# An encoder behind an expert attention on one core: the opening overlapped, the weights in five parts, and a new order of each engine's work in a slot

## What is computed

```
n = layer_norm(x0)
e = n + experts(n)            # 8 heads; a quarter of the rows each uses the first 128, 64, 32, 16 values
x = n
for i in range(4):
    q, k, v = split(layer_norm(x) @ Wi.T + bi)
    scores = q @ k.T / sqrt(8) + mask     # 16 heads, causal, with bias
    x = x + softmax(scores) @ v @ Wo.T + bo
    h = gelu(layer_norm(x) @ W1.T + b1)
    x = x + h @ W2.T + b2
return x0 + layer_norm(x) + e
```

## Time and profile before

| | us |
|---|---|
| Runs: median (lowest to highest) | 1649.23 (1647.62 to 1650.16) |
| Profiled execution: its own time | 1640.9 |
| Profiled execution: first to last instruction (span) | 1639.1 |
| PE busy / PE weight loads busy | 1421.8 / 946.2 |
| ACT busy | 1223.2 |
| DVE busy | 1131.8 |
| POOL busy | 614.3 |

### The profile page before, as it was taken

How to read it: one execution, slowest core, us unless ns; L and a number is a source line. 1 busy time by engine, 2 the same in 40 slices (tenths; PEclk the granted TensorE clock), 3 DMA queues, 4 the chain that set the end, 5 groups by cost and what they waited for, 6 DMA issues and landing times.

```text
span 1639.1 us, 38563 instructions
## 1 busy us (share of the span) xinstructions
PE 1421.8 (87%) x10720; PEld 946.2 (58%) x10720; DVE 1131.8 (69%) x2851; ACT 1223.2 (75%) x2165; POOL 614.3 (37%) x1052
## 2 busy tenths in 40 slices
PE   0677787568999999999999999999999989999995
PEld 0445554335666666666666666666666656666653
DVE  6567676347777777677677766777776767777762
ACT  3233333238999898898999888999888988888884
POOL 5232222123333343333333333334333345555443
PEclk9999888779999999999999999999999999999997
DMA  3332333045444444444444445444444444444430
GB/s 107 100 114 89 107 92 101 24 122 149 121 124 127 117 116 126 134 129 119 120 129 119 122 121 133 129 119 121 127 119 123 129 128 125 124 125 125 123 90 10
DMA packets 104789, 187.60 MB, mean 114 GB/s; under 512 B 19912, under 2 KB 70728, under 8 KB 104720
## 3 DMA queue, kind: packets, MB, share of 16 engines
q1 hardware_dynamic: 89904, 150.45, 33.3%
q0 software_dynamic: 14848, 36.72, 8.3%
HBM read 120.87 MB, written 65.01 MB: 113 GB/s over the span
## 4 chain that ended last, share of the span: by engine, by line
PE 53%; DVE 17%; issue 14%; DMA 9%; POOL 2%; DVEq 1%; ACT 1%; SPq 1%; POOLq 0%; ACTq 0%
PE pvp L979 11%; PE exp_ps L956 7%; DVE negm L698 6%; PE mxp L923 6%; PE dense L1009 6%; PE dense L1018 5%; PE dense L868 5%; DMA blocks<-split_L 4%; PE mxp L927 4%; DVE xn L666 3%; PE dense L896 2%; PE dense L997 2%; DVE ost L744 2%; PE mxp L868 2%; DMA blocks<-negt 2%
## 5 line engine op out<-in xcount | busy, mean ns | idle before, releaser
L831 ACT ACTIVATE probs<-exp_ps 128x512 f32<-128x512 f32 x896 | 525.0, 593 | 289.1 <-PE exp_ps L956 286.4
L698 DVE TENSOR_REDUCE negm<-mxp 128x2 f32<-128x512 f32 x896 | 569.2, 683 | 90.3 <-PE mxp L927 72.6
L956 PE MATMUL exp_ps<-qbd_l,kst_l 128*128 128x512 f32 x768 | 368.5, 495 | 8.3 <-issue 4.3
L923 PE MATMUL mxp<-blocks,qst 104*128 104x512 f32 x768 | 325.5, 453 | 34.5 <-DMA blocks<-split_L 19.7
L855 ACT ACTIVATE exp_ps<-masktf 128x512 f32<-128x512 f32 x513 | 308.8, 602 | 22.6 <-DVE rest L766 6.5
L927 PE MATMUL mxp<-maskb,identb 128*128 128x256 bf16 (+1 forms) x768 | 247.6, 322 | 0.0
L498 POOL TENSOR_SCALAR veps<-mv 128x2 f32<-128x2 f32 x144 | 31.7, 220 | 560.9 <-DVE mv L657 557.2
L923 PEld LDWEIGHTS mxp<-blocks,qst 104*128 104x128 f32 x768 | 149.0, 194 | 84.2 <-DVE negm L698 37.0
L979 PE MATMUL pvp<-probs,vst_l 128*32 128x256 f32 (+1 forms) x4096 | 194.5, 330 | 0.6 <-ACT probs L831 0.6
L744 DVE COPY ost<-pvp 128x512 f32<-128x512 f32 x80 | 55.3, 692 | 201.6 <-PE pvp L979 201.6
L956 PEld LDWEIGHTS exp_ps<-qbd_l,kst_l 128*128 128x128 f32 x768 | 144.4, 195 | 40.8 <-issue 31.3
(11 more groups left out here) (95 smaller groups left out, 2006.6 us busy)
## 6 DMA issues: line engine op xcount, KB each, us to landing
split_L<-hi SPq DMA_DIRECT2D x256, 128.0 KB, 2.1
qst<-split_L SPq DMA_DIRECT2D x64, 384.0 KB
kst_l<-split_L SPq DMA_DIRECT2D x64, 384.0 KB
qbd_l<-split_L SPq DMA_DIRECT2D x256, 96.0 KB
split_L<-lo POOLq DMA_DIRECT2D x128, 128.0 KB, 2.1
blocks<-split_L SPq DMA_DIRECT2D x128, 96.0 KB
blocks<-split_L POOLq DMA_DIRECT2D x128, 96.0 KB, 4.4
split_F<-hi SPq DMA_DIRECT2D x64, 128.0 KB, 2.1
```

What stands on the lines that cost most here:

```text
L698: dve.tensor_reduce(heads[:, g, first:first + count], mxp[:, (plan.max_chunks * g + ch) % 3, :].rearrange("p (h t) -> p h t", h=count), AX ...
L831: act.activation(probs[:, g[0], ch, :], exp_ps[:, (plan.exp_chunks * g[0] + ch) % 2, :], ACT.Exp, scale=plan.scale).then_inc(q.b_exp, 1)
L923: pe.matmul(mxp[:, bank, :], qst[0:BIAS_END, g[0], qt * P:(qt + 1) * P], kbd[0:BIAS_END, first:first + count, g[0], 0:keys], start=True, s ...
L956: pe.matmul(exp_ps[:, bank, :], kst[plan.name][:, s, g[0], kt * P:(kt + 1) * P], rhs, start=not on_diagonal, stop=True, skip_group_check=T ...
```

## The change

Nothing is computed otherwise, and the instructions that compute are the same in number (one memset of a single column goes). Four things change.

1. **The order in a slot.** `slot_steps` of the encoder is rewritten. Steps that several engines shared under one name are split, so that each engine's part has a place of its own: `qk+` into y (ACT), hi (DVE), lo (POOL), hi> (SP); `ln` into ln and rstd; `f1+` into two gelus; `f2` into two halves; `negt+` and `stack...` into the issuing engines' steps. The statistics and `xn` now belong to unit s+3, `v` stands at the end of the slot before, and the copy `pv+` is made one slot later. The maxima stand beside the exponentials 4 to 11, before beside 2 to 8.
2. **Banks.** Each transient result of PE has a bank of its own choice among five (`banks`), and a bank's reader is waited for by a helper (`take`).
3. **Weights in five parts**, each loaded as soon as its own last use is over; the first layer's are loaded at the start of the program. The columns of the two weight tiles are sorted to suit.
4. **The opening.** Before the last expert slots, each engine now runs the early steps of the encoder's first units (statistics of units 0 and 1, projections of unit 0). `blocks` is cleared after the last expert exponential, no longer after the last expert unit, and only some engines wait for the end of the experts.

```
         if self.causal:
             end, end2, store = (at(k, s - 2) if last_layer else [] for k in ("end", "end+", "store"))
             return (
-                exps[0:2] + at("ot", s - 1) + at("ln", s + 2) + at("ot+", s - 1) + at("v v+", s + 1) + at("xn", s + 2)
-                + at("f2 f2+", s - 2) + at("at at+", s - 1)
-                + exps[2:3] + maxes[0:2] + at("xt", s + 2)
-                + exps[3:4] + maxes[2:4] + at("xt+", s + 2) + at("op", s - 1) + at("stack+", s + 1)
-                + exps[4:5] + maxes[4:5] + at("op+", s - 1) + at("qk", s + 2)
-                + exps[5:6] + maxes[5:7] + at("qk+", s + 2)
-                + exps[6:7] + maxes[7:9] + at("xn2", s - 1) + end
-                + exps[7:8] + maxes[9:11]
-                + exps[8:9] + maxes[11:12]
-                + exps[9:10] + at("xt2 xt2+", s - 1) + values[0:2] + end2
-                + exps[10:11] + at("negt negt+", s + 1) + at("stack_max+", s + 2)
-                + exps[11:12] + at("f1 f1+", s - 1) + values[2:4] + at("pv+", s) + store)
+                at("rstd", s + 3) + part("f2", s - 2, 0) + at("ln", s + 3)
+                + part("exp", s, 0) + at("v+", s + 1) + at("w:v", s + 2)
+                + part("exp", s, 1) + at("ot pv+", s - 1) + part("f2", s - 2, 1) + at("w:w2 at+ ot+ at w=w1", s - 1)
+                + part("exp", s, 2) + at("stack>", s + 1) + at("xt", s + 2)
+                + part("exp", s, 3) + at("w=o op", s - 1) + at("hi>", s + 2) + at("row>", s + 1) + at("f2+", s - 2) + end
+                + part("exp", s, 4) + at("op+", s - 1) + part("max", s + 1, 0) + at("w=v xt+", s + 2) + part("pv", s, 0)
+                + part("max", s + 1, 1, 2) + at("w=w2", s - 1)
+                + part("exp", s, 5) + at("xn2", s - 1)
+                + part("exp", s, 6) + part("max", s + 1, 3, 4) + at("smax> qk y", s + 2) + at("w:qk", s + 3)
+                + part("exp", s, 7) + at("xt2", s - 1) + part("max", s + 1, 5) + at("xb xt2+", s - 1) + at("hi", s + 2)
+                + part("exp", s, 8) + part("max", s + 1, 6) + part("pv", s, 1) + part("max", s + 1, 7)
+                + part("exp", s, 9) + at("rstd2", s - 1) + part("max", s + 1, 8, 9) + end2 + part("max", s + 1, 10)
+                + part("exp", s, 10) + at("lo", s + 2) + part("max", s + 1, 11) + at("w=qk", s + 3)
+                + part("exp", s, 11) + part("gelu", s - 1, 0, 1) + part("f1", s - 1, 0) + at("negt negt+", s + 1)
+                + part("f1", s - 1, 1) + at("w:w1", s) + part("pv", s, 2) + at("smaxp", s + 2) + at("xn", s + 3)
+                + at("xb2", s - 1) + at("w:o", s) + part("pv", s, 3) + at("v", s + 2) + store)
...
+            if early is not None and early != (step in EARLY or step[0] == "w"):
+                continue
...
+ENCODER = Plan("L", 16, True, True, LAYERS * BATCH // 2, {
+    "xt": 1, "qk": 0, "v": 3, "at": 2, "op": 4, "xt2": 1, "negt": 2, "f2": 1, "ot": 4, "f1": (0, 1)})
+EARLY = ("ln", "rstd", "xn", "xt", "xt+", "qk", "y", "hi", "lo", "hi>", "v", "v+")
...
+WEIGHTS = {
+    "qk": ("a", A_Q, A_V), "v": ("a", A_V, A_COLS),
+    "o": ("c", C_O, C_W1), "w1": ("c", C_W1, C_W2), "w2": ("c", C_W2, C_COLS)}
...
+def wait_for_projections(eng, q):
+
+    for done in (q.a_rstd, q.a_xn, q.a_xt, q.a_mask, q.a_qk, q.a_v, q.a_hi, q.a_lo):
+        eng.wait_ge(done, EXPERT.units)
+    for s in range(2):
+        eng.wait_ge(q.parts[s], 16 * 4 * EXPERT.rounds)
+        eng.wait_ge(q.lo_parts[s], 16 * 2 * EXPERT.rounds)
+
+
+def expert_rounds(eng, experts, encoder, join):
+
+    experts(-1)
+    experts(0)
+    experts(1)
+    with eng.Fori(2, EXPERT.rounds - 1) as n:
+        experts(n)
+    experts(EXPERT.rounds - 1, slots=(0,))
+    join()
+    encoder(-2, early=True)
+    encoder(-1, slots=(0,), early=True)
+    experts(EXPERT.rounds - 1, slots=(1,))
+    experts(EXPERT.rounds)
+
+
+def encoder_opening(encoder, experts_done=None):
+
+    encoder(-2, early=False)
+    encoder(-1, slots=(0,), early=False)
+    if experts_done is not None:
+        experts_done()
+    encoder(-1, slots=(1,))
+    encoder(0)
+    encoder(1)
```

More of the change, by code:

```diff
@@ L114, in steps @@
+    def steps(self, n, last_layer=False, slots=(0, 1), early=None):
+        for step, off, *k in sum((list(self.slot_steps(s, last_layer)) for s in slots), []):
             u = 2 * n + off
+            if early is not None and early != (step in EARLY or step[0] == "w"):
+                continue
             if not isinstance(n, int) or 0 <= u < self.units:
-                yield step, u, off % 2, n + off // 2, g, off
-EXPERT = Plan("F", 8, False, False, BATCH // 2)
+                yield step, u, off % 2, n + off // 2, k[0] if k else 0, off
@@ L419, in load_c, with load_weights @@
-            def load_c(layer):
-                sp.wait_ge(q.c_done, BATCH * (layer + 1))
-                settle(sp, passed_sp)
-                sp.dma_start(wc["L"][:], wc_l[layer]).then_inc(q.wc, 16)
-                sp.wait_ge(q.wc, 16 * (layer + 1))
+            def load_weights(part, layer):
+                which, first, end = WEIGHTS[part]
+                to, source = (wa["L"], wa_l) if which == "a" else (wc["L"], wc_l)
+                sp.dma_start(to[:, first:end], source[layer][:, first:end]).then_inc(q.w[part], 16)
@@ L465, in _ @@
+            encoder_round(LAYERS - 1, 0)
+            encoder_round(LAYERS - 1, 1, last_layer=True)
+            with sp.Fori(2, per - 2) as k:
+                encoder_round(LAYERS - 1, k, last_layer=True, inner=True)
+            for k in range(per - 2, per + 1):
+                encoder_round(LAYERS - 1, k, last_layer=True)
             for s in range(2):
@@ L1023, in run @@
-            def run(plan):
-                read = [None, None]
-                def body(n):
-                    steps(plan, n, read)
-                    for k in range(2):
-                        if read[k] is not None:
-                            before, per_round, constant = read[k]
-                            read[k] = (before, per_round, constant - per_round)
-                rounds_of(pe, plan, body)
+                        o = take(at["f1"][k], q.c_gelu, NF, off, 2 * k + 2)
+                        for f in range(2 * k, 2 * k + 2):
+                            last = pe.matmul(o[:, (f % 2) * T:(f % 2 + 1) * T],
+                                             wc["L"][:, C_W1 + f * P:C_W1 + (f + 1) * P], xnt[:, 1, s, :],
+                                             start=True, stop=True)
@@ new lines, in next_round, with experts @@
+            def next_round(n):
+                for number, job in enumerate(read):
+                    if job is not None:
+                        before, per_round, constant = job
+                        loop_follows = not isinstance(n, int) or n == 1
+                        read[number] = ((before, per_round, constant - per_round) if loop_follows else
+                                        (before, 0, per_round * n + constant))
+            def experts(n, **part_of_round):
+                steps(EXPERT, n, **part_of_round)
+                next_round(n)
@@ L1036, in _, with encoder @@
+            def encoder(n, **part_of_round):
+                steps(ENCODER, n, **part_of_round)
+                next_round(n)
             pe.wait_ge(s_init, 12)
```

529 lines of the change are left out of this document (284 added, 245 removed).

## The result

| | before | after |
|---|---|---|
| Median of 4 runs each, us | 1648.4 (1644.1 to 1650.2) | 1679.7 (1672.5 to 1680.5) |
| Ratio to before, 95% interval | | 1.0181 [1.0153, 1.021] |
| Span of the profiled execution, us | 1639.1 | 1678.0 |

The kernel is 1.8% slower; the forecast was 1564.5, and the range ended at 1630. (A fourth run of the kernel before puts its median at 1648.4, for 1649.2 in the first table.) First the page of the changed kernel: its span, and the clock granted to TensorE in 40 slices, in tenths.

What follows compares the result with a forecast made beforehand. Each slot was DVE's stretch (10.37 us), then PE's queue (7.79), 18.26 with register rows; savings of 57.6 in three layers, 1.8 after unit 0, 13.7 in the last layer and 11.6 opening took 1649.2 to 1564.5; range 1525 to 1630.

Steps and rivals of the forecast that it cites:

- Each of the last 14 keeps its 0.94: 19.20 for 20.18: Last layer's 14 slots, with the final norm: each stays 0.94 us over a middle slot, together 13.7 us saved.
- The wait for the weights goes: Layer starts: weights in five parts arrive in time, leaving 3.0 of 6.6 us of other delays a layer.
- The slot: Encoder's middle slot: two stretches in turn plus 0.1 for register rows, 18.26 us, before 19.24.
- The DVE stretch: From the sum through the last maximum, DVE nearly without a break: work kept, left at 10.37 us.
- the other: From the last maximum to the next sum, set by PE's queue: 7.79 us, before 8.87.
- PE needs 17.5 and has little reserve: PE's work in a slot, priced from start to start: about 17.5 us, its busy 18.38 taken as overstated.
- Register arithmetic, 0.1: Added register rows for bank waits in PE's list: 0.1 us a slot, within bounds of nothing and 1.2.
- Opening: Encoder's start overlapping the last experts: first maximum 11.6 us earlier, near 323; bounds 5 to 19.
- the opening costs what it gives: Rival at the opening: join waits hold SP or POOL behind the experts; 73 us saved alone, 1576; 5%.
- ACT did not become the bound: Rival in the slot: ACT becomes the bound at 17.18 and 0.2 us, giving 1509; 12%.
- the drain beside a table load: ACT's table loads: a rule adds some 1380 ns drain each, ACT 19.9 a slot; the forecast took none.
- The rival on the other side: Slower rival: stacks come late at each slot's first maximum; with 1.9 us late, slot 20.2, time 1687; 8%.

Runs made afterwards that it cites:

- e3: Changed kernel with GpSimd's share of end moved behind xb and its share of end+ behind xb2: 1622.6 us, 0.9865 of the kernel before.
- e4: Changed kernel with weight part `o` loaded and released ahead of w1: 1666.5 us, 1.0126 of the kernel before.
- c5: Kernel with the three order edits (end, end+, `o` first), 8 of f2's 16 matmuls left out: 1598.4 us, 0.9696 of the kernel before.
- c3: Kernel with the three order edits, encoder maxima over every second key, exponentials scaled by 1/64: 1583.6 us, 0.9618 of the kernel before.
- d9: Kernel with the three order edits, each of the 12 mask products of a slot done twice: 1688.5 us, 1.0288 of the kernel before.
- e1: Changed kernel with only GpSimd's share of end+ moved behind xb2: 1666.6 us, 1.0131 of the kernel before.
- c2: Kernel with the three order edits, encoder's first steps moved back after the experts' last sum: 1604.3 us, 0.9752 of the kernel before.
- e2: Changed kernel with only GpSimd's share of end moved behind xb: 1672.7 us, 1.0164 of the kernel before.
- d6: Kernel with the three order edits, both every-second-key maxima (exponentials scaled by 1/64) and half of f2 left out: 1570.5 us, 0.9581 of the kernel before.

## Why the prediction was wrong

**The step that failed** is "Each of the last 14 keeps its 0.94: 19.20 for 20.18". The last layer's slots became 23.9. The final norm's work is the same, but POOL's parts of it moved ahead of xb and lo in its queue, and each waits there for DVE. The forecast carried the price over from the old order without asking what is queued behind `end` and `end+` in the new one. With both moved back (e3) the 13 slots behind the layer's first take 19.6 each, nine of them 19.2 to 19.5: the forecast 19.20 was nearly right for that order. 52 us of the result hang on this, enough to turn its sign.

**"The wait for the weights goes"** failed too. Over units 17 to 49, (1316.46 - 696.49) / 2 is 310.0 a layer; 16 slots of 18.89 are 302.2, so 7.8 us of other delays remain, for 3.0 forecast. The five parts didn't remove the wait but put `o`'s release behind w1 and the stacks' DMAs in SP's queue. With `o` first (e4) the copies to ost of units 17 and 49 are at 693.21 and 1302.84, 304.8 a layer: 2.6 of other delays, so 3.0 fits a kernel with `o` released in time.

**The slot**, forecast 18.26, is 18.89. The DVE stretch was right (10.43 for 10.37), the other mis-sized: 8.49 for 7.79. PE's pieces there are the ones I listed, but the sum has PE's prices alone, as if PE never waited in the stretch. It waits at the transposes of ost and of attn, each of which follows DVE's row by about 0.13: v+ and the copy to ost, and then the division, lie on the chain beside PE's pieces. From start to start the four exponentials take 1.41 for 0.96, f2 2.06 for 1.80, v 0.57 for 0.44, and op with its hand-over 0.80 for 0.54; the hand-over and transpose of the maxima take 0.35 for 0.6, and the transpose of ost 0.49 for 0.66. The four exponentials and f2 contain the waits. By c5, which takes half of f2 out and leaves this stretch at 8.48, f2's own work isn't what sets it. The other fault is "PE needs 17.5 and has little reserve". Prices from one start to the next were taken as what PE needs, and the 18.4 of its busy time as overstated. In c3, with DVE's maxima halved, the slot still took 18.81 with PE busy 98.5% of it, and in d9 added matmuls cost their full time, so the busy row was the better guide. "Register arithmetic, 0.1" can't be judged; no run shows it apart.

**Opening.** The first copy to ost is 8.4 us earlier, for 11.6, and in e1 to e4 2.8 to 8.9 earlier, so the size of the gain is uncertain. The inserted steps cost the experts 12.3 in the changed kernel (last sum at 323.38, before at 311.06) and 11.2 by c2, for a forecast 7.3; the first maximum on DVE is at 329.40, not near 323. c2 shows no gain from the overlap that stands clear of the difference between executions. The rival "the opening costs what it gives" is nearer to what the time shows. The slot after unit 0, forecast 1.8 shorter, was 4.9 longer, by the same release of `o` (24.0 to 18.2 in e4).

**What held.** ACT did not become the bound (364.99 of 400, its wait for scores 23.6, 1.1 a slot, under the 1.2 of the forecast), so the drain beside a table load is as absent here (0.4 us of idle time ahead of 21 loads) as in the earlier trace rows. The rival on the other side named late stacks in every slot; in the middle layers they were in time. In the last layer they were late, but not through that loop: POOL made lo 5 us late behind `end+`. Its sign was right, its place and its reason were not.

## What to carry to other kernels

Walk a new order once for every variant of the loop, the last iteration's above all, and for each step that waits write down what is queued behind it on its engine and who waits for that: two harmless looking places on the least loaded engine (36% busy) cost 3% here. A split release helps only if no other wait or DMA stands ahead of it in the queue that gives it. When an engine's busy time in a slot is 95% of the slot, take it as the floor until a run says otherwise; in a sum along one engine's list, ask at each piece that reads another engine's result when that result is there; and when two limits lie within 1% of each other, test an edit together with one that relieves the other.

## What the runs showed of the hardware

I had not expected waits on PE to be paid a second time. With the same 148 or 149 matmuls in a slot PE's busy time was 18.7 and 18.8 us at a granted clock of 1.00 and 21.3 at 0.86 and 0.87 (e2). The changed kernel's first slots of a layer, in which PE waits for `o`, had 0.93, 0.86 and 0.87 and 19.9 to 21.2 us of busy time; with `o` first (e4) they had 1.00 and 19.0. The middle layers as a whole, with PE idle 3 to 5% of the time, before and after the change, stayed at 1.00, and with both of POOL's waits gone (e3) the last layer behind its first slot had 1.00 as well. That the waits bring the clock down is read from these pairs; no run sets it apart. Twelve more small matmuls cost 0.127 us each (d9). Halving the elements of a maximum took its reduction from 0.69 to 0.43 us (c3's and d6's timelines), so part of a reduction's time doesn't depend on its size, unless reading every second element is slower, which no run shows apart.
